# Preparing and streaming the last feed forward layer of a two layer decoder on Trainium2

## The chip, the cores and the metric

The kernel runs on one core of a Trainium2 chip. The metric is the device time of one launch in microseconds (us). The five engines with their own instruction streams are TensorE (PE in the profile, its weight loads PEld), VectorE (DVE), ScalarE (ACT), GpSimd (POOL) and SyncE (SP), which issues most transfers.

## What is computed

X holds 16 batches of 256 tokens of 128 features, 4096 tokens. Six sublayers follow each other, and each ends as x = layernorm(x + f(x)):

```
x = _layernorm(x + _L0_attn_ref(x, ...))     # self attention, 16 heads of 8
x = _layernorm(x + _L0_xattn_ref(x, ctx, ...))   # cross attention over 1601 keys of 96
x = _layernorm(x + _L0_ffn_ref(x, ...))      # experts
x = _layernorm(x + _L1_attn_ref(x, ...))     # state space
x = _layernorm(x + _L1_xattn_ref(x, ctx, ...))   # cross attention over the same keys
x = _layernorm(x + _L1_ffn_ref(x, ...))      # feed forward, below
```

The last one, which the change is mostly about, is a layer of 128 -> 512 -> 128 with quantised weights and a lora term:

```
scale = max(|W|) / 127                       # one for each of W_fc, W_proj
Wq = W + ((clip(round(W / scale), -128, 127) * scale) - W)
h = gelu(x @ Wq_fc.T + b_fc + 2 * (x @ A_fc.T) @ B_fc.T)
y = h @ Wq_proj.T + b_proj + 2 * (h @ A_proj.T) @ B_proj.T
```

## The kernel before, in words

X lies in SBUF for the whole program as 32 tiles of 128 tokens x 128 features. The program is a row of blocks, and at the end of each all engines meet. `constants` (L689) loads X in four transfers of 512 KB and makes the identities on GpSimd; its block ends when X is there. `attention` (L158) runs three times: over 256 keys of the batch itself, and twice over the 1601 keys of the context. `experts`, `state_space` and `feed_forward` (L1357) follow their attentions, and `store` (L716) writes X with one transfer.

**Attention.** A static plan (`_schedule`, L76) gives each step of a batch a slot, and every engine walks through the same plan, each picking its own steps. The batches overlap: while a batch has its scores computed (B, L493) and weighted (PV, L514), the next has its queries and keys projected (Q, K, V). Those are split into three bf16 parts (SPLIT_Q, SPLIT_K, `split`, L272; on VectorE for batch 0, on GpSimd for the others). SP writes the parts to a stacked layout by nine transfers for queries, and nine per group of keys (STACK_Q, STACK_K, L333 to L360). Row maxima come from a first set of scores (A, L461), reduced by VectorE (L649), split by GpSimd (L401 to L407), transposed (MT, L485) and inserted as rows of the queries (ROWS). BIAS (L408) adds the bias of the output projection to a batch of X on GpSimd, OX, ONT, OUT and LN end the batch. The queues of all engines are in order. SP's first steps in an attention are the weights (L318 to L324) and LOAD_X of batches 0 and 1 (L329); GpSimd's are the constants and the stacks' fill (L370 to L377).

**Feed forward.** SP loads the raw weights and small tensors by eight transfers (L1415). TensorE transposes all 32 tiles of X (L1440), and ScalarE copies them to `xT` (L1491). VectorE takes the peaks of both weights (L1518), GpSimd spreads them over the partitions (L1428), and VectorE quantises in six passes (L1522 to L1528). TensorE transposes the quantised weights by products with the identity and adds the lora products into the same bank (L1453 to L1460), and ScalarE copies the result (L1496, L1498). Then come eight blocks of 512 tokens (`block_of`, L1465): four products for the hidden features (L1469), a product of a row of ones with the bias (L1474), Gelu on ScalarE (L1503), 16 products for the output (L1479). VectorE adds X (L1533) and normalises (`layernorm`), with the root on GpSimd (L1432, L1434). The first block is written out, the others are a hardware loop:

```
pe.matmul(bank[:, m, :], w1[:, m * P:(m + 1) * P], xb, start=True, stop=True)
...
pe.wait_ge(ln_dve, (i - 1) * (1 + 3 * BT) + 1)
...
pe.matmul(bank[:, 4, t * D:(t + 1) * D], ones_row[:, :], bias2[:, :],
          start=(t == 0), stop=False, skip_group_check=True)
...
pe.wait_ge(gelus, i * FC + m + 1)
```

## Time and profile before

| | us |
|---|---|
| median of 3 runs (3863.64 to 3867.38) | 3864.87 |
| the profiled execution | 3866.06 |
| its span, first to last instruction | 3864.3 |
| self attention and what is ahead of it | 0 to 335 |
| first cross attention | to 1752 |
| experts | to 2108 |
| state space | to 2351 |
| second cross attention | to 3753.3 |
| feed forward and store | to 3864.3 |

Over the span TensorE is busy for 89%, VectorE for 74%, ScalarE for 60%, GpSimd for 28%. A stretch's row gives busy time of each engine in it and the clock that TensorE was granted, as a share of 2.4 GHz (0.50 is 1.2 GHz). A timeline's row gives the start, the duration, engine, line and operation, out<-in by the program's names, the number of instructions merged into it, and in brackets how long the engine was idle before it and for whom. Times are from the start of the span.

### The profile page before, as it was taken

The page shows a single profiled execution, that of the slowest core. Times are in us where ns is not written, and L with a number is a line of the kernel's source. Part 1 is how long each engine was busy: PE and PEld are TensorE (multiplying, and loading weights), DVE is VectorE, ACT ScalarE, POOL GpSimd, SP SyncE. Part 2 cuts the span into 40 slices and gives each one's busy share as a digit, 9 for nine tenths or more (in the row PEclk, how much of TensorE's full clock was granted, in tenths as well). Part 3 has the DMA queues.
Part 4 walks back from the last instruction along what each step waited for, and adds up shares of the span by engine and source line. Part 5 has one row for each costly group of instructions (what it writes and reads, how often), then busy time and mean ns, then how long its engine had stood idle before and what let it go on. Part 6 is the DMA issues. An engine that isn't in the chain of part 4 may idle for free. (4 is left out here: it accounts for less than half of the span.)

```text
span 3864.3 us, 97882 instructions
## 1 busy us (share of the span) xinstructions
PE 3442.3 (89%) x39003; PEld 1703.8 (44%) x39003; DVE 2871.3 (74%) x3920; ACT 2329.9 (60%) x4575; POOL 1067.8 (28%) x1874
## 2 busy tenths in 40 slices
PE   5885999999999999984999582999999999999988
PEld 3442444444444444433666581444444444444435
DVE  5776788888888888854344896888888888888852
ACT  3663677777777777771332530777777777777663
POOL 4552223222222322201665002232222223222201
PEclk9997999999999999996999795999999999999998
DMA  3332222232222223201000002222322222232200
GB/s 98 75 79 58 61 55 60 55 77 61 56 63 54 59 58 75 57 12 25 1 0 1 0 0 61 53 60 56 76 63 54 63 54 59 62 70 63 49 16 22
DMA packets 165138, 194.88 MB, mean 50 GB/s; under 512 B 32166, under 2 KB 124123, under 8 KB 164715
## 3 DMA queue, kind: packets, MB, share of 16 engines
q1 hardware_dynamic: 164714, 189.03, 20.8%
q8 instruction: 291, 4.77, 0.5%
q14 instruction: 133, 1.08, 0.1%
HBM read 27.88 MB, written 2.10 MB: 8 GB/s over the span
## 5 line engine op out<-in xcount | busy, mean ns | idle before, releaser
L586 ACT ACTIVATE cross_Pr<-cross_sT 128x512 f32<-128x512 f32 (+1 forms) x3584 | 1833.6, 563 | 768.8 <-PE cross_sT L508 767.8
L649 DVE TENSOR_REDUCE cross_nm<-cross_ring 128x2 f32<-128x802 f32 x2048 | 1975.6, 991 | 323.7 <-PE cross_ring L474 295.3
L508 PE MATMUL cross_sT<-cross_Q,cross_K 64*128 64x256 bf16 x13312 | 1044.2, 273 | 49.3 <-ACT cross_Pr L586 42.2
L527 PE MATMUL cross_oT<-cross_Pr,cross_V 128*9 128x256 f32 x13312 | 1029.8, 381 | 0.0
L508 PEld LDWEIGHTS cross_sT<-cross_Q,cross_K 64*128 64x128 bf16 x13312 | 511.1, 95 | 771.8 <-ACT cross_Pr L586 637.1
L474 PE MATMUL cross_ring<-cross_K,cross_Q 64*128 64x401 bf16 x4096 | 662.3, 337 | 62.2 <-DMA cross_K<-cross_kparts 33.5
L401 POOL TENSOR_TENSOR cross_mp<-cross_nm,cross_one 128x8 bf16<-128x8 f32 x128 | 25.9, 202 | 1373.6 <-DVE cross_nm L654 1373.6
L527 PEld LDWEIGHTS cross_oT<-cross_Pr,cross_V 128*9 128x9 f32 x13312 | 197.6, 88 | 412.6 <-issue 245.1
L474 PEld LDWEIGHTS cross_ring<-cross_K,cross_Q 64*128 64x128 bf16 x4096 | 199.0, 94 | 202.7 <-DVE cross_nm L649 106.9
L1104 DVE TENSOR_TENSOR moe_rc<-moe_r,moe_bank 128x512 f32<-128x512 f32 x128 | 87.9, 687 | 170.8 <-ACT moe_r L995 170.8
L876 POOL TENSOR_TENSOR moe_hh<-moe_r,moe_rc 128x512 f32<-128x512 f32 x128 | 162.5, 1270 | 160.0 <-DVE moe_rc L1104 159.3
L995 ACT ACTIVATE moe_r<-moe_bank 128x512 f32<-128x512 f32 x144 | 86.1, 598 | 196.1 <-PE moe_bank L934 193.8
L586 ACT ACTIVATE self_Pr<-self_sT 128x512 f32<-128x512 f32 x256 | 138.8, 594 | 84.6 <-PE self_sT L508 84.4
L658 DVE TENSOR_REDUCE self_nm<-self_ring 128x4 f32<-128x1024 f32 x128 | 155.3, 1224 | 46.0 <-PE self_ring L481 41.8
L946 PEld LDWEIGHTS moe_bank<-moe_down,moe_hh 128*128 128x128 f32 x1152 | 150.7, 191 | 55.0 <-issue 47.1
L1245 PE MATMUL ssm_bank<-ssm_diag,ssm_state 128*128 x1024 | 124.0, 281 | 56.8 <-DVE ssm_state L1343 56.8
L276 POOL TENSOR_TENSOR cross_qparts<-cross_qf,cross_one 128x256 bf16<-128x256 f32 x30 | 18.4, 612 | 514.3 <-DVE cross_qf L626 514.3
L946 PE MATMUL moe_bank<-moe_down,moe_hh 128*128 128x128 f32 x1152 | 152.4, 275 | 0.0
L934 PE MATMUL moe_bank<-moe_xT,moe_up 128*128 (+1 forms) x288 | 149.4, 601 | 1.3 <-ACT moe_cT L988 1.3
L1245 PEld LDWEIGHTS ssm_bank<-ssm_diag,ssm_state 128*128 128x128 f32 x1024 | 120.2, 196 | 60.6 <-issue 52.4
L458 PE MATMUL cross_ring<-cross_wv,cross_in 97*128 97x128 f32 (+1 forms) x832 | 124.1, 296 | 21.0 <-DVE cross_nm L649 21.0
L1343 DVE TENSOR_TENSOR_SCAN ssm_state<-ssm_decay,ssm_dtu 128x2048 f32<-128x2048 f32 x32 | 139.2, 4411 | 4.7 <-PE ssm_bank L1245 2.7
(296 smaller groups left out, 3035.7 us busy)
## 6 DMA issues: line engine op xcount, KB each, us to landing
cross_K<-cross_kparts SPq DMA_DIRECT2D x1152, 100.1 KB, 2.3
cross_in<-in_ctx_T_dram SPq DMA_DIRECT2D x32, 600.4 KB, 5.5
self_QK<-self_parts SPq DMA_DIRECT2D x144, 128.0 KB, 2.7
cross_Q<-cross_qparts SPq DMA_DIRECT2D x288, 64.0 KB, 2.1
X<-in_x_dram SPq DMA_DIRECT2D x4, 512.0 KB, 6.1
self_in<-in_x_T_dram SPq DMA_DIRECT2D x16, 128.0 KB, 2.3
cross_Q<-cross_mst SPq DMA_DIRECT2D x128, 16.0 KB, 1.8
out_dram<-X SPq DMA_DIRECT2D x1, 2048.0 KB, 8.7
```

The lines of the kernel that those rows point to most:

```text
L458: mm = pe.matmul(R[0:r, (c - lo) * D:(c - lo + 1) * D], sT_in[b % 2][:, s:s + r], wv[:, :], start=True, stop=True)
L474: mm = pe.matmul(R[:, 512 * j:512 * j + cfg.block], Q[ROWS * j:ROWS * (j + 1), pair, 0, t * P:(t + 1) * P], K[ROWS * j:ROWS * (j + 1), pai ...
L508: mm = pe.matmul(sT[0:r, cfg.sT_bank(b, u + j), (c % 2) * S:(c % 2 + 1) * S], K[ROWS * j:ROWS * (j + 1), pair, t, s:s + r], Q[ROWS * j:ROW ...
L527: mm = pe.matmul(oT[32 * j:32 * j + VR, 0:S], V[0:r, b % VB, c, 4 * g + j, :], Pr[0:r, slot, (c % 2) * S:(c % 2 + 1) * S], start=(c == 0), ...
L586: act.activation(Pr[0:r, u % NPR, 0:nc_ * S], sT[0:r, cfg.sT_bank(b, u), 0:nc_ * S], ACT.Exp).then_inc(exped, 1)
L649: dve.tensor_reduce(nm4[:, g % 2, t, :, pk, blk], R.rearrange("p (j n) -> p j n", j=2)[:, :, 0:cfg.block], AX.X, ALU.max, negate=True).the ...
L658: dve.tensor_reduce(nm[:, g % 2, :, :, a].rearrange("p t j -> p j t"), R.rearrange("p (j t n) -> p j t n", j=2, t=QT), AX.X, ALU.max, nega ...
L876: pool.tensor_tensor(hh[:, q, :], r[:, q, :], rc[:, q, :], ALU.mult).then_inc(hidden, 1)
L934: pe.matmul(bank[:, m % 2, :], up[:, m, :], xb, start=True, stop=True).then_inc(up_done, 1)
L946: mm = pe.matmul(bank[:, 4, t * D:(t + 1) * D], hh[:, m % 3, t * P:(t + 1) * P], down[:, m, :], start=(m == 0 and t == 0), stop=(m == NCH ...
L1245: return pe.matmul(bank[:, tile // BT, (tile % BT) * D:(tile % BT + 1) * D], lhs, rhs, start=first and tile % BT == 0, stop=True, skip_gro ...
L1343: dve.tensor_tensor_scan(state[:, h, :], decay[:, h, :], dtu[:, h * HALF:(h + 1) * HALF], 0.0, ALU.mult, ALU.add).then_inc(scanned, 1)
```

## The change

There are five parts; the 16 output products of a block stay as they are. The line numbers of the changed kernel differ by those added.

1. X is loaded in the self attention: two transfers of 1024 KB on SP's queue, one behind each of LOAD_X of batch 0 and 1. The first BIAS on GpSimd waits for both. `constants` loads nothing.
2. The host lays out the last layer's weights: both transposed in one tensor, the four lora matrices in another, the bias by partition. ScalarE issues the loads of both tensors in the second cross attention, behind the XT of batch 0.
3. The quantisation moves into the second cross attention: peaks on VectorE (OX of batch 4), their spreading and scaling on GpSimd (BIAS of batch 6), the reciprocal on VectorE (OX of batch 8), and the six passes over each of the two weights on GpSimd, two per BIAS of batches 9 to 14.
4. The last layer transposes a block of X one block ahead, adds the bias on GpSimd to X, copies transposed X by VectorE, adds the lora product to the weights on VectorE, has two banks for its output, and is written out without loops. A Gelu of one column comes first on ScalarE.
5. Each block of 512 tokens is stored as soon as it is normalised, and there is no block for the store.

```
@@ attention, sync @@
                         sp.dma_start(sT_in[b % 2][0:KIN, :], src_T[b]).then_inc(in_ready[b % 2], 16)
+                        if x_dram is not None and b < 2:
+                            n = NT // 2
+                            sp.dma_start(X[:, b * n:(b + 1) * n, :],
+                                         x_dram.rearrange("b (t p) f -> p (b t) f", p=P)[:, b * n:(b + 1) * n, :])\
+                              .then_inc(x_in, 16)
@@ attention, gpsimd, BIAS @@
+                        else:
+                            pool.wait_ge(x_in, 16 * 2)
...
+                        if ffn_weights is not None and b == 6:
+                            ffn_spread(ffn_weights, pool)
+                        if ffn_weights is not None and 9 <= b < 15:
+                            ffn_quantise(ffn_weights, pool, (b - 9) // 3, (b - 9) % 3)
@@ attention, scalar, XT @@
+                        if ffn_weights is not None and b == 0:
+                            ffn_load(ffn_weights, act)
@@ attention, vector, OX @@
+                        if ffn_weights is not None and b == 4 and half == 0:
+                            ffn_measure(ffn_weights, dve)
+                        if ffn_weights is not None and b == 8 and half == 0:
+                            ffn_invert(ffn_weights, dve)
@@ constants @@
-            for q in range(4):
-                n = NT // 4
-                sp.dma_start(X[:, q * n:(q + 1) * n, :],
...
-            sp.wait_ge(x_in, 16 * 4)
@@ new functions @@
+def ffn_load(fw, act):
+    weights, lora = fw.dram
+    act.dma_start(fw.raw[:, :, :], weights).then_inc(fw.loaded, 16)
+    act.dma_start(fw.lora[:, :], lora).then_inc(fw.lora_loaded, 16)
+def ffn_measure(fw, dve):
+    dve.wait_ge(fw.loaded, 16)
+    dve.tensor_reduce(fw.peak[:, :], fw.raw[:, :, :], AX.X, ALU.max, apply_absolute_value=True)\
+       .then_inc(fw.measured, 1)
+def ffn_spread(fw, pool):
+    pool.wait_ge(fw.measured, 1)
+    pool.partition_all_reduce(fw.peaks[:, :], fw.peak[:, :], P, bass.bass_isa.ReduceOp.max)\
+        .then_inc(fw.peaked, 1)
...
+def ffn_quantise(fw, pool, w, part):
...
+    if part == 0:
+        pool.wait_ge(fw.measured, 2)
+        pool.tensor_tensor(quant, raw, inverse, ALU.mult).then_inc(done, 1)
+        pool.wait_ge(done, n + 1)
+        pool.tensor_scalar(quant, quant, ROUND, -ROUND, ALU.add, ALU.add).then_inc(done, 1)
...
@@ feed_forward, sync @@
+            for i in range(NBLK):
+                sp.wait_ge(ln_dve, (i + 1) * PER)
+                sp.dma_start(out.rearrange("b (t p) f -> p (b t) f", p=P)[:, i * BT:(i + 1) * BT, :],
+                             X[:, i * BT:(i + 1) * BT, :]).then_inc(stored, 16)
+            sp.wait_ge(stored, 16 * NBLK)
@@ feed_forward, gpsimd, per block @@
+                pool.wait_ge(turned, i + 1)
+                pool.tensor_tensor(xb, xb, bias2[:, :].unsqueeze(1).broadcast_to([P, BT, D]), ALU.add)\
+                    .then_inc(biased, 1)
+                pool.wait_ge(ln_dve, i * PER + 1 + 2 * BT)
@@ feed_forward, tensor @@
+            pe.wait_ge(fw.lora_loaded, 16)
+            pe.matmul(bank[:, 5, :], lora[:, 0:D], lora[:, D:D + F], start=True, stop=True).then_inc(lora_done, 1)
+            turn(0)
+            for c in range(FC):
+                mm = pe.matmul(bank[:, 4, c * D:(c + 1) * D], lora[:, D + F + c * P:D + F + (c + 1) * P],
+                               lora[:, D + 2 * F:2 * D + 2 * F], start=True, stop=True)
...
+            for i in range(NBLK):
+                pe.wait_ge(took, i + 1)
+                for m in range(FC):
+                    pe.matmul(bank[:, m, :], w[:, 0, m * P:(m + 1) * P], xT[:, i % 2, :], start=True, stop=True)\
+                      .then_inc(hidden, 1)
+                if i + 1 < NBLK:
+                    turn(i + 1)
...
+                if i >= 2:
+                    pe.wait_ge(ln_dve, (i - 2) * PER + 1)
...
@@ feed_forward, vector @@
+            dve.wait_ge(fw.quantised, 12)
+            dve.wait_ge(lora_done, 1)
+            dve.scalar_tensor_tensor(w[:, 0, :], bank[:, 5, :], SCALING, fw.quant[:, 0, :], ALU.mult, ALU.add)\
+               .then_inc(w_ready, 1)
+            take(0)
...
+            for i in range(NBLK):
+                if i + 1 < NBLK:
+                    take(i + 1)
+                dve.wait_ge(summed, i + 1)
+                dve.wait_ge(biased, i + 1)
...
```

What moves stands in the instruction orders. SP at the start of the program, before (`x_T` is X transposed for the projections):

```order
L699 DMA X<-in_x_dram 128x8x128 x4
L694 UNCONDITIONAL_BRANCH [waits x_in]
L315 UNCONDITIONAL_BRANCH [waits barrier_Pool_Activation_PE_DVE_SP_release]
L320 DMA self_wq<-in_self_wq_dram 128x128
L320 DMA self_wk<-in_self_wk_dram 128x128
L320 DMA self_wv<-in_self_wv_dram 128x128
L320 DMA self_wo<-in_self_wo_dram 128x128
L323 DMA self_bq<-in_self_bq_dram 128x1
L324 DMA self_bo<-in_self_bo_dram 128x128
L332 DMA self_in<-in_x_T_dram 128x256 x2
L358 DMA self_QK<-self_parts 16x16x256 [waits self_split_k,self_rows_set]
```

The same place in the change:

```order
L321 DMA self_wq<-in_self_wq_dram 128x128
L321 DMA self_wk<-in_self_wk_dram 128x128
L321 DMA self_wv<-in_self_wv_dram 128x128
L321 DMA self_wo<-in_self_wo_dram 128x128
L324 DMA self_bq<-in_self_bq_dram 128x1
L325 DMA self_bo<-in_self_bo_dram 128x128
L333 DMA self_in<-in_x_T_dram 128x256
L336 DMA X<-in_x_dram 128x16x128
L333 DMA self_in<-in_x_T_dram 128x256
L336 DMA X<-in_x_dram 128x16x128
L364 DMA self_QK<-self_parts 16x16x256 [waits self_split_k,self_rows_set]
```

The four loads of X and the wait for them are gone from the front, and two loads stand between and behind the inputs of batch 0 and 1, ahead of the first stacking.

GpSimd in the second cross attention around the BIAS of batch 9, before:

```order
L405 TENSOR_TENSOR cross_mp<-cross_mres,cross_one 128x4x2
L407 TENSOR_TENSOR cross_mp<-cross_mres,cross_mp 128x4x2
L412 TENSOR_TENSOR X<-X,cross_bo 128x256
L276 TENSOR_TENSOR cross_qparts<-cross_qf,cross_one 128x256
L278 TENSOR_TENSOR cross_res<-cross_qf,cross_qparts 128x256
```

And in the change:

```order
L411 TENSOR_TENSOR cross_mp<-cross_mres,cross_one 128x4x2
L413 TENSOR_TENSOR cross_mp<-cross_mres,cross_mp 128x4x2
L420 TENSOR_TENSOR X<-X,cross_bo 128x256
L1413 TENSOR_TENSOR ffn_quant<-ffn_raw,ffn_inverse 128x512
L1415 TENSOR_SCALAR ffn_quant<-ffn_quant 128x512
L277 TENSOR_TENSOR cross_qparts<-cross_qf,cross_one 128x256
L279 TENSOR_TENSOR cross_res<-cross_qf,cross_qparts 128x256
```

Two passes of the quantiser stand between the bias and the split of the next queries; five more batches have two each at the same place.

TensorE in the last layer of the change, from its first instruction into the second block (`ident_f` as input: the transposes; before, all 32 of them stood first):

```order
L1507 MATMUL ffn_bank<-ffn_lora 128x512
L1502 MATMUL ffn_bank<-ident_f,X 128x128 x4
L1510 MATMUL ffn_bank<-ffn_lora 128x128 x4
L1517 MATMUL ffn_bank<-ffn_xT,ffn_w 128x512 x4
L1502 MATMUL ffn_bank<-ident_f,X 128x128 x4
L1528 MATMUL ffn_bank<-ffn_w,ffn_g 128x128 x16
L1517 MATMUL ffn_bank<-ffn_xT,ffn_w 128x512 x4
L1502 MATMUL ffn_bank<-ident_f,X 128x128 x4
L1528 MATMUL ffn_bank<-ffn_w,ffn_g 128x128 x16
```

The products with the bias are gone, and the transposes of the next block stand between the two sets of products.

## Rows read from the trace of the kernel before

**Rows 1.** Table of stretches: TensorE, weight loads, VectorE, ScalarE, GpSimd busy, clock, DMA.
```profile
30.00:342.00 312.00, 245.27 (x3028) 139.36 (x3028) 217.39 (x366) 180.99 (x401) 158.37 (x432) 0.98 0.28 70
...
2351.00:3753.00 1402.00, 1322.16 (x16320) 568.40 (x16320) 1128.17 (x1431) 960.38 (x1952) 343.36 (x612) 0.98 0.25 59
3753.00:3864.00 111.00, 87.88 (x453) 63.43 (x453) 33.10 (x123) 38.67 (x52) 10.24 (x19) 0.84 0.09 25
```

**Rows 2.** Timeline of the start: start, duration, engine, line, operation, [idle before].
```profile
0.72 4.04 SPq L699 DMA_DIRECT2D X<-in_x_dram  x4
...
1.70 0.29 POOL L712 TENSOR_SCALAR_AFFINE_SELECT ident_b<-ident_b 128x128 bf16<-128x128 bf16 x1
10.57 0.35 SPq L320 DMA_DIRECT2D self_wq<-in_self_wq_dram  x1
...
16.55 1.19 PE L443 MATMUL self_ring<-self_in,self_wq 128*128 128x256 f32 x2 [16.55 <-DMA self_in<-in_x_T_dram]
...
22.44 5.94 SPq L358 DMA_DIRECT2D self_QK<-self_parts  x9
...
30.43 1.03 PE L481 MATMUL self_ring<-self_QK 64*128 64x256 bf16 x8 [6.46 <-DMA self_QK<-self_parts]
```

**Rows 3.** Timeline of the last layer before its blocks, columns as in rows 2.
```profile
3753.62 6.31 PE L1440 MATMUL ffn_bank<-ident_f,X 128*128 128x128 f32 x32 [3.33 <-PEq L161]
...
3755.60 0.60 ACT L1491 ACTIVATE ffn_xT<-ffn_bank 128x512 f32<-128x512 f32 x1 [0.26 <-PE ffn_bank L1440]
...
3758.78 1.22 DVE L1518 TENSOR_REDUCE ffn_peak<-ffn_raw 128x2 f32<-128x1024 f32 x1 [5.47 <-DMA ffn_bias<-in_L_ffn_b_proj_dram]
...
3768.25 0.77 PE L1453 MATMUL ffn_bank<-ident_f,ffn_quant 128*128 128x128 f32 x2 [7.77 <-DVE ffn_quant L1528]
...
3780.55 6.55 PE L1469 MATMUL ffn_bank<-ffn_xT,ffn_w 128*128 128x512 f32 x8 [0.69 <-ACT ffn_w L1498]
...
3788.11 3.84 PE L1479 MATMUL ffn_bank<-ffn_w,ffn_g 128*128 128x128 f32 x32
```

**Rows 4.** Timeline of a block, of the last sum and of the store.
```profile
3791.79 3.60 PE L1469 MATMUL ffn_bank<-ffn_xT,ffn_w 128*128 x8
3792.12 0.69 DVE L1533 TENSOR_TENSOR ffn_y<-ffn_bank,X 128x512 f32<-128x512 f32 x1 [24.01 <-PE ffn_bank L1479]
...
3795.32 1.15 PE L1474 MATMUL ffn_bank<-ffn_bias,ones_row 1*128 1x128 f32 x8
...
3796.40 3.84 PE L1479 MATMUL ffn_bank<-ffn_w,ffn_g 128*128 128x128 f32 x32
...
3850.12 0.69 DVE L1533 TENSOR_TENSOR ffn_y<-ffn_bank,X 128x512 f32<-128x512 f32 x1 [3.69 <-PE ffn_bank L1479]
...
3853.60 1.12 DVE L1143 TENSOR_SCALAR X<-ffn_y,ffn_mv,ffn_rstd 128x128 f32 x4 [1.40 <-POOL ffn_rstd L1434]
3855.17 0.41 SPq L721 DMA_DIRECT2D out_dram<-X  x1
```

**Rows 5.** Table of stretches, columns as in rows 1: the two rises of the clock.
```profile
3758.00:3759.00 1.00, 1.00 (x7) 1.00 (x6) 0.22 (x1) 0.60 (x1) 0.00 (x0) 0.50 0.15 2
...
3786.00:3787.00 1.00, 1.00 (x3) 0.17 (x1) 0.00 (x0) 0.69 (x1) 0.00 (x0) 0.84 0.00 0
```

**Rows 6.** DMA issues by size: count, KB each, us to landing.
```profile
X<-in_x_dram SPq DMA_DIRECT2D x4, 512.0 KB, 6.1
self_in<-in_x_T_dram SPq DMA_DIRECT2D x16, 128.0 KB, 2.3
...
out_dram<-X SPq DMA_DIRECT2D x1, 2048.0 KB, 8.7
```

**Rows 7.** Costliest groups: count, busy us, mean ns, idle before.
```profile
L876 POOL TENSOR_TENSOR moe_hh<-moe_r,moe_rc 128x512 f32<-128x512 f32 x128 | 162.5, 1270 | 160.0 <-DVE moe_rc L1104 159.3
```

**Rows 8.** Waits in the second cross attention: us in total, times, longest.
```profile
POOL cross_qparts L276 <- DVE cross_qf L626: 256.9, 15, 17.9
...
ACT cross_mst L572 <- PE cross_ring L490: 43.4, 1, 43.4
```

More of the change, by code:

```diff
@@ L713, in _ @@
                                    pattern=[[-1, P]], channel_multiplier=1).then_inc(set_, 1)
-def store(nc, ctx, X, out):
-    stored = ctx.enter_context(nc.semaphore("stored"))
-    with nc.Block() as block:
-        @block.sync
-        def _(sp):
-            sp.dma_start(out.rearrange("b (t p) f -> p (b t) f", p=P), X[:, :, :]).then_inc(stored, 16)
-            sp.wait_ge(stored, 16)
 T = B * S
@@ L1359, in feed_forward @@
+def feed_forward(nc, top, X, ident_f, fw, b_fc, b_proj, out):
     with ExitStack() as ctx:
@@ L1473, in block_of @@
-                for t in range(BT):
-                    pe.matmul(bank[:, 4, t * D:(t + 1) * D], ones_row[:, :], bias2[:, :],
-                              start=(t == 0), stop=False, skip_group_check=True)
+                if i + 1 < NBLK:
+                    turn(i + 1)
+                if i == 0:
+                    pe.wait_ge(w_ready, 2)
+                if i >= 2:
+                    pe.wait_ge(ln_dve, (i - 2) * PER + 1)
                 for m in range(FC):
@@ L1527, in _, with take @@
-            link(dve.tensor_tensor(flat(tmp), flat(quant), flat(raw), ALU.subtract))
-            link(dve.tensor_tensor(flat(quant), flat(tmp), flat(raw), ALU.add))
-            assert steps[0] == QSTEPS
-            per = 1 + 3 * BT
-            with dve.Fori(0, NBLK) as i:
+            def take(i):
+                dve.wait_ge(turned, i + 1)
+                dve.tensor_copy(xT[:, i % 2, :], bank[:, 6 + i % 2, :]).then_inc(took, 1)
+            dve.wait_ge(fw.quantised, 12)
+            dve.wait_ge(lora_done, 1)
```

208 lines of the change are left out of this document (91 added, 117 removed).

## The prediction

> **What bounds the kernel now.** The table of stretches is read first [rows 1]. The 111 us of the last layer hold 88 us of TensorE work at a mean granted clock of 0.84, while the second cross attention before it has TensorE busy for 94% (1322.16 of 1402 us). So TensorE sets the pace in both. The timeline of the start comes next [rows 2]: nothing computes until the loads of X have landed, the second stage's first load is issued at 10.57 us, and TensorE begins 5.98 us later. The timeline of the last layer [rows 3] shows three parts: 38.5 us from its first transpose (3753.62) to the first sum on VectorE (3792.12); seven blocks of (3850.12 - 3792.12)/7 = 8.29 us [rows 4]; a tail of 14.2 us to the end of the span (3864.3). In a block [rows 4] TensorE has no gap: 3.53 us of up-projection (3791.79 to 3795.32), 1.08 of bias (to 3796.40) and the remaining 3.68 of down-projection. The clock rows [rows 5] say why the first part is dear: TensorE is at 0.50 (1.2 GHz) until 3759, and again from its idle wait for the quantiser until about 3786.5.
>
> The sum is made against the profiled execution, 3866.06 us outside and 3864.3 us of span. That is 1.19 us over the median of the three runs, 3864.87.
>
> **The start.** X no longer holds back the first block. GpSimd's last constant starts at 1.70 us and takes 0.29 [rows 2], so the next stage can begin near 2.4 instead of 10.57 us: 8.2 us. Its chain is unchanged in length: weights, projection, splits, stack. In SP's queue the two halves of X now lie between the loads of batch 0 and 1, and ahead of the first stacking transfers (22.44 us before, 14.3 now). The whole output, 2048 KB, lands in 8.7 us, and a quarter of X in a median of 6.1 with three more in the queue [rows 6]. An issue takes 0.35 to 0.41 us [rows 2, 4], so behind six loads of weights and one of input X is issued from about 5.5 us on, and its 2 MB are through by about 5.5 + 8.7 = 14.2, when the stacking data would only begin to move. I take **8.0** us. The ends are 8.2, and 8.2 less the half of X that might still be in the way, 4.3 us, so 3.9.
>
> **GpSimd inside the second cross attention.** Six times it gets two passes over 128x512 elements right behind the bias of a batch. A pass is nowhere in the trace in this form; the nearest row, a two-input float product of the same shape, takes 1.27 us [rows 7], so 2.5 us a step. The next thing in GpSimd's order is the split of the next queries, and for that it waited 256.9 us in 15 batches, 17.1 us each [rows 8]. The steps end over 14 us before that. The reduction over partitions and its scaling, once, lie in the same gap. I cost all at **0**. The Trainium skill (GPSIMD Engine Reference, Engine selection) says to keep elementwise work on VectorE, GpSimd being about twice as slow on two inputs. By that the move should lose: were its twelve passes on the path, 12 x 1.27 = 15 us would come back onto the sum. The trace has a wait in their place, so they are not.
>
> **VectorE and ScalarE inside it.** VectorE gets one reduction of 128x1024, 1.22 us in the stage now [rows 3], and one tiny reciprocal. TensorE may stand still behind them or have other work. Between 0 and 1.4 us; I take **0.5** lost. ScalarE issues two transfers just after it has emptied the first transposed queries, and its next instruction waited 43.4 us and more [rows 8]. Their 592 KB need under 3 us at the rate of the output's store, and lie between the context's load and the stacks. I cost that at nothing; were the stacks hit, it would be those 3 us at most.
>
> **The preparation of the last layer.** Gone are 28 of the 32 transposes ahead of it, the wait for eight loads, the quantiser's chain and 16 small products at 1.2 GHz. What is left in front of the first up-projection is one lora product of 512 columns, four transposes and four lora products of 128. A product of 512 columns has two passes: 6.55 us for eight passes at 1.2 GHz with their end, near 0.85 a pass [rows 3], so 1.7. Four transposes: the copies behind them come every 0.60 + 0.26 = 0.86 us [rows 3], so 0.85. The four small products have no row in this order. The sixteen products of the stage now take (3780.55 - 3768.25)/16 = 0.77 each with their last copy [rows 3], so 3.0 at most; if their weight loads overlap, as they do in the block, two passes of 0.21 are 1.7. I take 2.7, nearer to the row. Together 5.3 us, from 3753.6 to 3758.9. VectorE meanwhile adds the first weights (0.69) and copies the first block (0.69), which end near 3757.1, so TensorE is the later one. The first up-projection depends on the clock. In this stage it rose at 3759 after 5.4 us of unbroken work from 3753.62, and near 3786.5 after 6 us of it from 3780.55 [rows 3, 5]. If the new work from 3753.6 counts as unbroken, all eight passes run at 2.4 GHz and end at 3762.4. If only the projection does, six and a half run at 1.2 and it ends at 3765.1. Then four transposes at 0.43 and the down-projection with its latency, 4.01 (3788.11 to 3792.12): the first sum starts at 3766.8 or 3769.5. I take the middle, 3768.2, which is **23.9** earlier; the ends are 22.6 and 25.3. ScalarE loads its table for Gelu while that goes on.
>
> The Trainium skill (TensorE: Matmul & The Clock Gate, What's actually happening) says that the monitor's window runs free of the kernel, so the point of the rise varies from run to run. The two rises above, 5.4 and 6 us after the start of work, do not contradict it. Both ends stay in by the rows alone.
>
> **Seven blocks.** The bias products go (1.08) and four transposes of the next block come (0.43, not in the last block). From first to last sum: 7 x (3.53 + 3.68) + 6 x 0.43 = 53.05 instead of 58.00, so **4.95** less. The cover: VectorE needs 4.60 us from sum to written X (3850.12 to 3853.60 + 1.12) [rows 4], a copy of 0.69 and the waits, about 5.4 of the 7.64 us. GpSimd needs 1.4 for the root and 1.3 for the bias addition, which comes after the root and ends some 3 us before it is wanted. If that cover went, VectorE would have 2.2 us to lose first.
>
> **The end.** Now the store is issued 0.45 us after the last X and lands 8.7 us later. In the change seven of eight parts are stored under the blocks, and the last, 256 KB, follows the wait after some 0.15 us. Its landing is bounded by 2.3 (128 KB of input) and 6.1 (512 KB in a queue) [rows 6]. Scaling the store's 7 us of data to an eighth and keeping its other 1.7 to 2 us gives 2.8. Saved: 9.15 - 2.95 = **6.2**; with the ends 6.7 and 2.9.
> The Trainium skill (DMA: Bandwidth & Descriptors, Measured) wants transfers of 1 MiB or more. By that eight small stores would be a loss; in line, seven more fixed parts of 1.7 us would be 12 us. But each has 7.64 us before the next.
>
> **The sum.** 8.0 + 23.9 + 4.95 + 6.2 - 0.5 = 42.6 us. 3866.06 - 42.6 = 3823.5 for the profiled run, 3822.3 against the median.
>
> **The rivals.**
> 1. *The start gives its gain back.* The halves of X sit in front of batch 1 and the stacks, and the self attention waits for them, or the stage turns out to be paced by later transfers. For it: all go through one queue. Against: SP's next issue after its first loads is only at 22.44 us now, so the 2 MB have the time to pass. It costs 4 to 8 us: 3826 to 3830.
> 2. *The inserted steps disturb the cross attention.* GpSimd's order is fixed, so a slow step delays the split of queries and of maxima, and TensorE stops at the transposed maxima. With 17.1 us of cover that takes passes of over 8 us; short of that a VectorE instruction that is slowed beside GpSimd could cost 1 us or so in each of six batches. Total 3824 to 3840.
> 3. *Slower.* The clock is lost in the self attention. There TensorE had 245 of 312 us of work at a clock of 0.98 [rows 1], though it once waited 6.46 us for the stacks [rows 2]. In the last layer a wait of 7.77 us was followed by 1.2 GHz [rows 3]. If with work beginning 8 us sooner the clock falls at the first gap and does not come back, the 245 us become about 490 in a stage of 312, that is 0.57 us lost per us of stage. From 75 us at 1.2 GHz on, the whole 42.6 is gone; with the whole stage it is about 4000. Against it: the last layer, once dense, regained 2.4 GHz twice within about 6 us [rows 5].
> 4. *The change doesn't do what it says:* the last layer stays as long per block, because VectorE, with a copy more, or the GpSimd bias becomes the bound. Then the 4.95 go and perhaps 5 more: 3827 to 3832.
>
> **How the numbers follow.** The forecast has 0.76, rival 1 0.08, rival 2 0.08, rival 3 0.03, rival 4 0.05. The number is the forecast's, 3822.3. All good ends together give 3819.7 (0.2 + 1.4 + 0.5 + 0.5 less), all bad ends 3831.9 (4.1 + 1.3 + 3.3 + 0.9 more). Shifts of phase in two stages of 1400 us, which I can't cost, could be 2 us either way. So the range is 3817 to 3831, which takes in the forecast, most of rival 1 and parts of rivals 2 and 4. A measurement can tell 0.2%, about 7.7 us, from no change. Faster by more than that: 0.95. Within: 0.02, a bad rival 2 or a small rival 3. Slower: 0.03.
>
> **What would show it.** Right: a first instruction of TensorE near 8.4 us; a first VectorE sum in the last layer 14 to 16 us after its first matmul; blocks of 7.64 us; a last store landing in under 3.5 us; second cross attention within 2 us of 1402. Wrong: waits of TensorE or ScalarE for self attention's stacks longer than now; GpSimd's quantising steps ending less than 5 us ahead of the split of queries; a block over 8 us; a granted clock at 0.50 inside the self attention.

## The result, and the profile after

The changed kernel took 3814.25 us (median, 3813.41 to 3819.08), the kernel before, run beside it, 3864.26 (3857.27 to 3867.38). The ratio is 0.9876, 95% interval 0.9859 to 0.9893: faster by 1.2%, some 50 us where 42.6 were predicted. The profiled execution took 3814.54 us with a span of 3812.7, against 3866.06 and 3864.3: 51.5 us.

Both spans can be cut at the same instructions. Stage by stage, from the start times in the two timelines (us; a last X is the row of the last tiles of X that VectorE writes in a stage):

| stage, by its first and last instruction | before | after | less |
|---|---|---|---|
| to TensorE's first projection | 16.55 | 8.45 | 8.1 |
| to the first scores of self attention | 13.88 | 15.05 | -1.2 |
| rest of self attention | 311.93 | 312.85 | -0.9 |
| first cross attention, to its last X | 1396.16 | 1394.63 | 1.5 |
| to the experts' first transpose of X | 14.35 | 12.02 | 2.3 |
| experts | 355.7 | 351.5 | 4.2 |
| state space, to its last sum | 237.4 | 237.1 | 0.3 |
| second cross attention, to its last X | 1407.0 | 1406.8 | 0.2 |
| preparation, to the last layer's first sum | 39.1 | 15.3 | 23.8 |
| to its eighth sum | 58.0 | 51.7 | 6.3 |
| to the end of the span | 14.2 | 7.3 | 6.9 |

The stretches of the changed kernel that answer to [rows 1]; columns: TensorE, its weight loads, VectorE, ScalarE, GpSimd busy, clock, DMA share, GB/s.

```profile
23.00:336.00 313.00, 245.18 (x3028) 139.05 (x3028) 217.24 (x366) 181.04 (x401) 158.50 (x432) 0.99 0.27 69
2337.00:3738.00 1401.00, 1321.91 (x16320) 567.96 (x16320) 1128.16 (x1431) 960.82 (x1952) 358.21 (x622) 0.98 0.26 59
3738.00:3813.00 75.00, 66.32 (x362) 47.33 (x362) 39.07 (x124) 23.48 (x34) 19.93 (x27) 0.91 0.11 30
```

The attentions have the same work at the same clock, with 15 us more of GpSimd in the second cross attention; the last layer has shrunk from 111 to 75 us. The start (against [rows 2]):

```profile
2.57 0.40 SPq L321 DMA_DIRECT2D self_wq<-in_self_wq_dram  x1
...
6.03 0.85 SPq L336 DMA_DIRECT2D X<-in_x_dram  x1
6.93 1.98 SPq L333 DMA_DIRECT2D self_in<-in_x_T_dram  x1
8.45 1.19 PE L455 MATMUL self_ring<-self_in,self_wq 128*128 128x256 f32 x2 [8.45 <-DMA self_in<-in_x_T_dram]
9.12 0.71 SPq L336 DMA_DIRECT2D X<-in_x_dram  x1
...
14.32 5.97 SPq L364 DMA_DIRECT2D self_QK<-self_parts  x9
...
23.50 1.04 PE L493 MATMUL self_ring<-self_QK 64*128 64x256 bf16 x8 [7.65 <-DMA self_QK<-self_parts]
```

The last layer, whose row of TensorE answers to [rows 3] and [rows 4]:

```profile
3739.03 2.04 PE L1507 MATMUL ffn_bank<-ffn_lora 16*128 16x512 f32 x2 [3.32 <-PEq L161]
...
3741.00 1.11 PE L1502 MATMUL ffn_bank<-ident_f,X 128*128 128x128 f32 x4
...
3742.04 2.07 PE L1510 MATMUL ffn_bank<-ffn_lora 16*128 16x128 f32 x8
...
3744.04 5.62 PE L1517 MATMUL ffn_bank<-ffn_xT,ffn_w 128*128 128x512 f32 x8
...
3749.93 3.74 PE L1528 MATMUL ffn_bank<-ffn_w,ffn_g 128*128 128x128 f32 x32
...
3753.50 3.60 PE L1517 MATMUL ffn_bank<-ffn_xT,ffn_w 128*128 128x512 f32 x8
3753.70 0.69 DVE L1562 TENSOR_TENSOR ffn_y<-ffn_bank,X 128x512 f32<-128x512 f32 x1 [2.88 <-PE ffn_bank L1528]
...
3756.94 0.60 PE L1502 MATMUL ffn_bank<-ident_f,X 128*128 128x128 f32 x4
3757.13 1.27 POOL L1491 TENSOR_TENSOR X<-X,ffn_bias 128x512 f32<-128x512 f32 x1
...
3810.06 0.37 SPq L1478 DMA_DIRECT2D out_dram<-X  x1
```

TensorE works without a gap from 3739.03. In the stretch that answers to [rows 5] its clock rises at about 3747.9, 8.9 us later:

```profile
3747.00:3748.00 1.00, 1.00 (x2) 0.44 (x2) 0.00 (x0) 0.14 (x1) 0.00 (x0) 0.54 0.03 8
3748.00:3749.00 1.00, 1.00 (x3) 0.38 (x2) 0.00 (x0) 0.71 (x2) 0.00 (x0) 1.00 0.00 0
```

### The profile page after: what moved, and what is told of

Same layout as the page of the kernel before. It is cut to its first block and busy times, and to the rows that moved or that the text cites. A ratio compares the mean times of both kernels' runs of the same rounds, so it can differ in the third digit from the quotient of the medians.

```text
span 3812.7 us, 97480 instructions
## 1 busy us (share of the span) xinstructions
PE 3414.2 (90%) x38912; PEld 1681.8 (44%) x38912; DVE 2877.0 (75%) x3923; ACT 2315.7 (61%) x4557; POOL 1093.5 (29%) x1895
## 5 line engine op out<-in xcount | busy, mean ns | idle before, releaser
L520 PE MATMUL cross_sT<-cross_Q,cross_K 64*128 64x256 bf16 x13312 | 1043.8, 273 | 48.6 <-ACT cross_Pr L600 42.6
L277 POOL TENSOR_TENSOR cross_qparts<-cross_qf,cross_one 128x256 bf16<-128x256 f32 x30 | 18.4, 613 | 486.0 <-DVE cross_qf L640 486.0
```

The lines of the kernel that those rows point to most:

```text
L520: mm = pe.matmul(sT[0:r, cfg.sT_bank(b, u + j), (c % 2) * S:(c % 2 + 1) * S], K[ROWS * j:ROWS * (j + 1), pair, t, s:s + r], Q[ROWS * j:ROW ...
```

## The experiments

"Beside" names the kernel before, run on the same chip.

**How much is noise.** The kernel before, unchanged.

> The kernel before, unchanged, to see what one more profiled execution of the same instructions shows. From the first transpose of the first cross attention to the last X of the second one, the trace of before has 3410.6 us and that of the change 3402.0. Own theory: that stretch varies from execution to execution (where the clock rises, how long the experts' weights take to land), and here it is between 3400 and 3412, not equal to 3410.6. Rival: it is fixed by the kernel, so 3410.6 within 1 us, and the 8 us belong to the change.

3860.66 us; 18 executions of the kernel before there have a median of 3860.73 (3858.35 to 3867.61). In its profile the start, the preparation, the blocks and the tail agree with the table above within 0.2 us. Self attention took 2.9 us more, the first cross attention 2.4 less, and the experts 351.5 and not 355.7. The stretch that I had asked about took 3402.4 us, against 3410.6 in the trace of before and 3402.0 in the change's, so the rival (3410.6 within 1) fell: those stages vary by themselves. The changed kernel, once more:

> The change once more, for the comparison on the same chip. Own theory: 46 to 48 us less than before as timed beside it, 50 being what the first reference runs showed by their place in their spread; from its own stages, start 8.1, experts' weights 2.4, preparation 23.7, blocks 6.3, tail 6.9, together 47.4. Rival: the whole 50 is the change's.

3819.10 us median (3814.54 to 3825.59), ratio 0.9892 (0.9875 to 0.9908), beside 3861.34: 42.2 us less, where I had expected 46 to 48. Preparation 15.3, blocks 51.7, tail 7.3 are again the same. Over both measurements the change is worth 42 to 50 us.

**The start.** Two kernels take this part alone: before with X loaded in self attention, and the change with X loaded at the front.

```
x_only:   +  sp.dma_start(X[:, b * n:(b + 1) * n, :], ...).then_inc(x_in, 16)     # behind LOAD_X, b < 2
          -  sp.wait_ge(x_in, 16 * 4)                                           # in constants
x_front:  the same two edits backwards, on the changed kernel
```

> The kernel before with only the load of X moved behind the first weights. Own theory: the first scores come 6.9 us earlier, the self attention ends 6 us earlier, and the time is 6 us less than before, 3858. Rival: an earlier start also makes the later stages shorter; then 14 us less, 3850. The prediction had 8.0 less, 3856.

> The change with the load of X put back ahead of everything, the rest as in the change. Own theory: 6 us more than the change, 3820. Rival (an earlier start shortens the later stages too): 14 more, 3828.

x_only 3853.01 us, ratio 0.9978 (0.9968 to 0.9988), 7.7 us under the 3860.73 beside it. x_front 3822.55, 8.3 over the change's 3814.25, where I had expected 6 in both; its first projection starts at 16.51 and its last layer is the change's (15.3, 51.7, 7.3). The start is worth 8 us both ways. Of what the first projection gains, 1 us is given back at the stacks. x_front:

```profile
30.68 1.04 PE L486 MATMUL self_ring<-self_QK 64*128 64x256 bf16 x8 [6.75 <-DMA self_QK<-self_parts]
```

From the first projection to this row x_front takes 14.17 us; the change takes 15.05 and x_only 15.09. The second half of X is issued only at 9.12, since the second input's issue, behind the first half, takes 1.98 us in place of about 0.45. It is still under way when the stacking begins. How long the second half of X and the first stacking transfer take to land in the change:

```profile
DMA to landing us min/median/max: 8.7/8.7/8.7
DMA to landing us min/median/max: 3.5/3.5/3.5
```

So X lands at 17.8 us, 3.5 behind the first issue for the stacks. In `better` (below), where X comes behind the stacks, they are issued as early and land sooner, and the scores start 0.9 us earlier:

```profile
DMA to landing us min/median/max: 2.5/2.5/2.5
14.35 5.98 SPq L360 DMA_DIRECT2D self_QK<-self_parts  x9
22.59 1.04 PE L494 MATMUL self_ring<-self_QK 64*128 64x256 bf16 x8 [6.72 <-DMA self_QK<-self_parts]
```

**The second cross attention.** Is GpSimd's wait really a cover? `dose` adds passes behind each quantising step, on scratch data that nothing reads: with the step's own two there are 12 in each of batches 9 to 11 and 24 in each of 12 to 14. `quant_dve` moves the quantiser to VectorE.

```
dose:       +  for k in range(22 if w else 10):
            +      pool.tensor_tensor(tmp, raw, inverse, ALU.mult).then_inc(fw.extra, 1)
quant_dve:  -  ffn_quantise(ffn_weights, pool, (b - 9) // 3, (b - 9) % 3)     # BIAS
            +  ffn_quantise(ffn_weights, dve, (b - 9) // 3, (b - 9) % 3)      # OX
```

> The change with more GpSimd work behind the bias of a batch in the second cross attention: 10 further passes of 1.27 us in batches 9 to 11 (12 in all, 15 us) and 22 further in batches 12 to 14 (24 in all, 30 us); the further passes write a scratch tensor. Own theory: up to about 17 us the work lies in GpSimd's wait for the next queries, so batches 9 to 11 keep their 84.03 us, and each of the last three gets longer by 30.5 - 17.1 less some slack, about 12 us. Rival: any GpSimd work there slows its neighbours; then batches 9 to 11 are longer by 1 us or more as well, and the two passes of the change cost a part of that.

> The change with the six passes over each weight on VectorE, at the first OX of batches 9 to 14, not on GpSimd. A pass over half the columns takes 0.69 us there with two inputs and about 0.4 with one, 7 us in all. Own theory: VectorE has some slack against TensorE, but the ring of two buffers passes on part of it: second cross attention 2 to 5 us longer than the 1406.8 of the change. Rival (from a page's rule that VectorE is the place for elementwise work): as short or shorter than with GpSimd.

dose: 3839.4 us. With 12 passes the batches follow each other at 84.03 us as without any; with 24 the stage is 1431.3 us instead of 1406.8, 8.2 for each of the three batches, where I had expected about 12. GpSimd's rows, first the change, then dose, at the next split of the queries:

```profile
3245.47 0.61 POOL L277 TENSOR_TENSOR cross_qparts<-cross_qf,cross_one 128x256 bf16<-128x256 f32 x1 [15.26 <-DVE cross_qf L640]
```

```profile
3230.70 11.12 POOL L1432 TENSOR_TENSOR ffn_tmp<-ffn_raw,ffn_inverse 128x512 f32<-128x512 f32 x10
3245.88 0.62 POOL L277 TENSOR_TENSOR cross_qparts<-cross_qf,cross_one 128x256 bf16<-128x256 f32 x1 [4.05 <-DVE cross_qf L640]
```

The wait shrinks by what is put in (15.26 to 4.05 us for ten passes of 1.11), and the path feels the passes only when it is used up. quant_dve: 3815.03 us, stage 1406.7 us. I had expected 2 to 5 us more, and that fell: VectorE is busy for 80% of the stage, but the twelve passes, 0.43 or 0.69 us each there, cost the stage nothing. So in this kernel the choice of the engine costs nothing either way.

**The blocks.** `bias_pe` puts the bias products back on TensorE and takes the addition on GpSimd out; `unroll` is the kernel before with the hardware loop written out.

```
bias_pe:  +  for t in range(BT):
          +      pe.matmul(bank[:, 4 + i % 2, t * D:(t + 1) * D], ones_row[:, :], bias2[0:1, :], ...)
          -  pool.tensor_tensor(xb, xb, bias2[:, :].unsqueeze(1).broadcast_to([P, BT, D]), ALU.add)
unroll:   -  with pe.Fori(1, NBLK) as i:
          +  for i in range(NBLK):
```

> The change with the bias of the second product by TensorE again (four products of a row of ones with it per block), none on GpSimd. Own theory: TensorE sets the pace, a block takes 7.45 + 1.08 = 8.5 us, first to last sum 51.7 + 7.5 = 59.2, and VectorE's first write of X falls from 1.3 to 0.34 us, since GpSimd's bias pass that ran beside it is gone. Rival: the block is bound by VectorE and GpSimd already; then under 3 us more.

> The kernel before with the eight blocks of the last layer written out on all engines, nothing else. Own theory: the hardware loop and its waits against a register cost TensorE 0.2 us a block (3.44 + 3.57 in the change against 3.53 + 3.68), so first to last sum is 58.0 - 1.4 = 56.6. Rival: the missing bias products free the two other pieces; then 58.0 as before.

bias_pe: 3827.86 us, 13.3 over the change's profiled execution: 4.7 before the first sum (20.0 for 15.3; TensorE also waits for the bias to land, and starts 4.1 us after the last X and not 0.7) and 9.0 over the blocks, 60.7 against 51.7. A block in it:

```profile
3766.58 3.60 PE L1513 MATMUL ffn_bank<-ffn_xT,ffn_w 128*128 128x512 f32 x8
...
3770.02 0.60 PE L1497 MATMUL ffn_bank<-ident_f,X 128*128 128x128 f32 x4
...
3770.55 1.15 PE L1522 MATMUL ffn_bank<-ffn_bias,ones_row 1*128 1x128 f32 x8
...
3771.63 3.84 PE L1527 MATMUL ffn_bank<-ffn_w,ffn_g 128*128 128x128 f32 x32
...
3775.30 3.60 PE L1513 MATMUL ffn_bank<-ffn_xT,ffn_w 128*128 128x512 f32 x8
```

From start to start: 3.44, 0.53, 1.08 and 3.67, together 8.72 us. The change's block is 3.44, 0.44 and 3.57 (3753.50, 3756.94, 3757.38 and on), 7.45. The bias products cost 1.08 themselves and 0.1 on either side, 1.27 in all. unroll: 3860.07 us, blocks 58.0 as with the loop, where I had expected 56.6. The loop costs nothing; that theory fell, and the borders of the bias products are what is left.

**The tail.** One store of everything behind the last block:

```
one_store:  -  sp.wait_ge(ln_dve, (i + 1) * PER)          # per block
            +  sp.wait_ge(ln_dve, NBLK * PER)             # once, then one dma_start of X
```

> The change with X stored by one transfer at the end. Own theory: only the tail changes, from last sum to the end 7.3 us becomes 4.60 + 0.15 + 8.7 + 0.4 = 13.9, 6.6 us more than the change. Rival: the seven stores under the blocks cost something there; then the blocks get shorter than 51.7 us by a microsecond or more and part of the 6.6 comes back.

3819.87 us, tail 13.7 us against 7.3, blocks 51.7. The blockwise stores take nothing from the blocks and are worth 6.4 us; the block boundary that also went is the other 0.4. The landings, change and one_store:

```profile
out_dram<-X SPq DMA_DIRECT2D x8, 256.0 KB, 2.3
```

```profile
out_dram<-X SPq DMA_DIRECT2D x1, 2048.0 KB, 8.7
```

**The 2.3 us that no part of the prediction has.** Between the first cross attention and the experts TensorE waits for the experts' weights, and the first transpose of X comes 14.4 us after the last X before and 12.0 after, with the same instructions. What differs is where the buffers lie: the change allocates 17440 B of each partition ahead of them. Six kernels are the one before with so much reserved: `pad` 17440 B, in eight buffers as in the change, then one buffer of 32, 1024, 8192 or 16384 B, and `pad128` with the four smallest of the eight, 8 B each.

```
pad:     +  for k, n in enumerate((1024, 1024, 1024, 1280, 2, 2, 2, 2)):
         +      sb(f"reserved{k}", [P, n], F32)
pad32:   +  sb("reserved", [P, 8], F32)             # the other sizes likewise
pad128:  +  for k in range(4):
         +      sb(f"reserved{k}", [P, 2], F32)
```

> The kernel before with 17 KB per partition reserved in SBUF where the change holds the last layer's weights; no instruction is added. Own theory: addresses cost nothing, so 3864 us within 4. Rival: the other addresses speed up stages that the change does not touch; then about 8 us less, 3856.

> The kernel before with 32 bytes per partition reserved ahead of all stages' tensors, where the change has 17440 bytes, which is 34 x 512 + 32. From the last X of the first cross attention to the first transpose of the experts, three kernels without the reserve show 14.26 to 14.38 us and three with it 11.83 to 12.02. Own theory: what counts is where the weights' rows start relative to some larger block, so 32 bytes do it: 11.9. Rival: the place in SBUF as such, 17 KB further, does it: 14.3.

> The kernel before with 1024 B of each partition reserved ahead of the working buffers, so that every buffer lies 1024 B further. Asked: what part of the shift by 17440 B makes the experts' first transposes come 11.8 to 12.4 us after the first cross attention's last X, and not 14.3 us. 32 B did nothing. Theory A, it is the place in the large (a boundary that the weights' buffers cross, at a distance of many KB): 14.3 here. Theory B, a low-order alignment between 32 B and 1 KB: 12 here.

> The same with 8192 B reserved. Theory A with a boundary less than 8 KB off: 11.9 us; with one further off: 14.3. Theory B (low-order alignment): as with 1024 B.

> The same with 16384 B reserved, 1056 B short of what the change reserves. Theory A (a boundary within 16 KB): 11.9 us from the last X to the experts' first transpose. Theory B (the 1056 B left over matter): 14.3 us, and 12 with 1024 B.

> The kernel before with four buffers of 8 B a partition reserved, which is the part of the 17440 B that is left without its four large buffers. 1024, 8192 and 16384 B left the wait for the experts' weights at 14.2 to 14.5 us (11.8 with all 17440 B). Theory A, the small buffers shift the weights' low-order address: 12 us here, and the transfer of the last part of the weights runs at about 340 GB/s and not at 217. Theory B, it takes the large part (over 16 KB): 14.3 us.

| | pad | pad32 | pad1024 | pad8192 | pad16384 | pad128 |
|---|---|---|---|---|---|---|
| last X to the experts' first transpose, us | 11.8 | 14.3 | 14.5 | 14.4 | 14.2 | 11.7 |
| time, us | 3860.18 | 3861.83 | 3858.53 | 3864.21 | 3860.25 | 3860.44 |

The four small buffers do it, the large ones don't, and 32 B, of which I had expected it, don't either. pad32 to pad128 are one execution each, but all traces of this case divide the same way: eight kernels without the small buffers have 14.2 to 14.6 us, twelve with them 11.7 to 12.4. One us in which the last part of the weights moves, pad32 and then pad128 (last column GB/s):

```profile
1748.00:1749.00 1.00, 0.00 (x0) 0.00 (x0) 0.00 (x0) 0.00 (x0) 0.86 (x2) 0.50 1.15 220
```

```profile
1748.00:1749.00 1.00, 0.00 (x0) 0.00 (x0) 0.00 (x0) 0.00 (x0) 0.82 (x1) 0.50 1.12 340
```

The queue is as full in both and moves half as much again. The totals don't show 2.3 us (pad's ratio is 0.9995, 0.9986 to 1.0005), since other stages vary by as much. That points to a low-order address of the destination: shifts by multiples of 1024 B and one by 32 B leave the long wait, four buffers of 8 B end it. The Trainium skill (DMA: Bandwidth & Descriptors, How a descriptor splits into AXI transactions) says that a transaction has to start at a multiple of 256 B, and that a descriptor that does not start there fetches bytes which it does not use; its example of 576 B takes one transaction more for it. It says so of reads, these are writes, and the addresses were not read out; if each small buffer takes 32 B, the buffers stood 128 B off such a multiple before and on it after, and every column of the table fits. That is argued, not shown.

**Can the clock of the last layer be held?** The preparation runs 8.9 us at 1.2 GHz. `better` moves X behind the first stacks, and adds 28 bf16 products of 64 rows behind the last output projection of the cross attention; `dense` and `dense14` leave X, and put float products of 128 rows (results unused) into all four waits at the end of the last batch.

```
better:   +  pe.matmul(sT[:, k % 3, 0:S], Ks[0][0:ROWS, 0, 0, 0:P], Qs[...][0:ROWS, 0, 0, :], ...)   # x28, behind OUT
dense:    +  pe.matmul(sT[:, j % 3, 0:P], ident_f[:, :], wo[:, :], start=True, stop=True)
             # x4 behind PV, x7 behind OX, x5 behind ONT, x28 behind OUT
dense14:     # the same, x2, x3, x2, x14
```

> The change with two more edits: the halves of X are loaded behind the stacks of batches 0 and 1 instead of between the first inputs, and TensorE gets 28 products into a free bank behind the last output product of the second cross attention, so that it does not stand idle into the last layer; their results are used nowhere. Own theory: the first scores come 0.5 to 1 us earlier; the last layer begins at 2.4 GHz and its first sum comes 10 to 11 us after the last X of the attention instead of 15.3. Together 5 us less than the change, 3809. Rival: the clock falls all the same or the filler delays the end of the attention; then no difference, 3814.

> The change with TensorE kept at work over the thin end of the second cross attention: in the last batch, 4 float products of 128 rows and 128 columns behind the last weighted values, 7 behind the transposes of the outputs, 5 behind those of the scaled outputs and 28 behind the output projection, into banks that nothing reads any more, so computation of the kernel is untouched. In the run of the better version 28 bf16 products of 64 rows came too late: the clock had gone to 0.50 at 3735, in the thin 3 us before them, they ran 6.2 us instead of 3, and the clock rose only 8.7 us after the first float product behind them, as in the change (8.9 us). Theory A: the clock falls because TensorE is thin from 3732 on, and work placed there holds it at 1.00: then the 8.9 us that the change runs at 0.50 in the last layer's preparation shrink by half, the first sum comes 10.5 to 11.5 us after the last X (15.3 in the change), and the time is 4 us under the change's, near 3810 to 3812. Theory B: the clock falls near there whatever these short products do; then the fillers run at 0.50 too, end some 3 us late as in the better version, the first sum comes 18 us behind, and the time is 3817 or more.

> As the dense version, with half the products: 2, 3, 2 and 14 in place of 4, 7, 5 and 28. There each product took 0.23 us in its two passes, the last 28 took 6.42 us where the wait they cover is 3.3, and held the last layer back by 3 us, though the clock stayed at 1.00 all through. Theory A (the clock is held by work over the thin end, and what is left is the overshoot): 14 products take 3.2 us and end with the last X; the second cross attention is 0.8 us shorter than with 28 (1406.8), the first sum of the last layer comes 11.0 to 11.5 us after it (14.3 with 28, 15.3 in the change), and the median falls to 3810 or 3811, 4 us under the change. Theory B (half the work is too thin to hold the clock): it falls near the end of the cross attention, and the first sum comes 15 us or more behind, 3814 or more.

better: 3815.62 us (3814.45 to 3818.48), ratio 0.9878 (0.9862 to 0.9895), first sum 18.4 us after the last X, 3.1 later than in the change. Its filler came too late:

```profile
3735.00:3736.00 1.00, 0.69 (x3) 0.71 (x4) 0.00 (x0) 0.17 (x1) 0.00 (x0) 0.50 0.00 0
```

```profile
3736.44 6.15 PE L567 MATMUL cross_sT<-cross_Q,cross_K 64*128 64x256 bf16 x28
3742.89 2.04 PE L1513 MATMUL ffn_bank<-ffn_lora 16*128 16x512 f32 x2 [0.30 <-PEq L162]
```

The clock was down before it began, and it ran into the last layer. Nor did it bring the clock back: that rose near 3751.9, 9.0 us after the first float product behind it, and 15.5 us after the filler's start. X behind the stacks made the first scores 0.9 us earlier (14.13 us) and is no gain over self attention. The waits in which the clock is lost begin before: in the change TensorE has 1.10 us of work from 3732 to 3735. dense: 3814.14 us (3812.35 to 3815.32), ratio 0.9881 (0.9864 to 0.9897). The clock is 1.00 all through, but each product has two passes of 0.115 us, so the last 28 took 6.42 us where 3.3 were to be covered, and the first sum is at 14.3 us, where I had expected 10.5 to 11.5. dense14:

```profile
3737.00:3744.00 7.00, 6.79 (x60) 5.99 (x52) 2.29 (x10) 0.77 (x2) 0.89 (x2) 1.00 0.00 0
3744.00:3755.00 11.00, 10.70 (x61) 7.46 (x61) 2.82 (x6) 4.24 (x6) 1.41 (x3) 1.00 0.04 9
```

The first sum comes 11.2 us after the last X, 4.1 under the change, as theory A had it. The whole time does not show it: 3814.07 us (3810.39 to 3816.27), ratio 0.9873 (0.9856 to 0.9889) beside 3861.89, where I had expected 3810 or 3811. The profiled execution has 355.2 us in the experts, 3.7 more than the change's, which takes the gain away. So dense14 beats the change in the stage it edits, and not measurably in the whole.

## Why the prediction was right, and where wrong

The direction was right, and so was the mechanism of each part but for one step at the start. The size was not: the forecast was 3822.3 with a range from 3817, and 3814.25 lies below it. The steps that failed are the terms for the blocks (4.95 us, measured 6.3) and for the end (6.2, measured 6.9), the 0.5 us of disturbance that did not come, the experts' weights, which had no term (2.3), and the time before that the sum is subtracted from, which was 3.9 us above what most executions take.

- **Start**, forecast 8.0, ends 3.9 and 8.2. Measured 8.1 to the first projection, 7.7 and 8.3 for the whole time in the two kernels that isolate it. The step "its 2 MB are through by about 5.5 + 8.7 = 14.2" failed: they landed at 17.8, after the first issue for the stacks at 14.32, and the scores came 1 us later for it. That is the part of rival 1 that came true.
- **GpSimd in the cross attention**, 0. Right, and for the passes shown by the dose: the twelve take 14.3 us (0.61 to 1.95 each). The split of the queries waits 228.9 us in 15 batches where it waited 256.9 [rows 8]. The other half of these 28 us is not the passes but the reduction over partitions, of which the prediction says no more than that it lies in the same gap. It did, with 3.9 us to spare out of 17.1, once:

```profile
2897.69 0.37 POOL L1401 PARTITION_ALL_REDUCE ffn_peaks<-ffn_peak  x1 [5.45 <-issue]
2905.16 0.25 POOL L1404 TENSOR_SCALAR ffn_scale<-ffn_peaks 128x2 f32<-128x2 f32 x1 [7.11 <-issue]
2909.31 0.61 POOL L277 TENSOR_TENSOR cross_qparts<-cross_qf,cross_one 128x256 bf16<-128x256 f32 x1 [3.90 <-DVE cross_qf L640]
```

  The two instructions are busy for 0.62 us, but from the end of the bias (2892.2) to the end of the scaling 13.2 us pass. What fills them the trace does not show. By the Trainium skill (GPSIMD Engine Reference, Engine selection) VectorE should be better for the passes. Each is shorter there (0.43 or 0.69 us), and the stage was the same within 0.1 us (quant_dve).
- **VectorE and ScalarE there**, 0.5 lost. Measured 0.2 gained, within what the stage varies by, so nothing. Rival 2 did not occur.
- **Preparation**, 23.9. Measured 23.8. The lead up to the first up-projection took 5.0 us (3739.03 to 3744.04) for 5.3. The first sum came 14.67 us after the first product, for 14.6. But the clock rose neither after 5.4 to 6 us of work nor that long after the projection began; it rose after 8.9, between the two, and the middle that I took was right by luck. This was not the chance of one execution: in ten traces of kernels with the old front the clock rises 4.8 to 5.6 us after the stage's first product, in seven with the new one 8.1 to 9.0, wherever it had fallen (1.2 to 5.0 us ahead of that product in the ten, 1.3 to 8.3 in the seven). The old front is 6.3 us of transposes with 128 rows; the new one has 2 us of products with 16 rows, 1 us of such transposes and 2 us of products with 16 rows again. Whether the 16 rows delay the rise was not tried.
- **Blocks**, 4.95. Measured 6.3. The term was mis-sized in "the bias products go (1.08)": I took the start-to-start times 3.53 and 3.68 of the neighbours over unchanged, and both had 0.1 us in them that belonged to the bias products. Seven blocks are shorter by 1.27 each, and six of them longer by the new transposes (0.44).
- **End**, 6.2. Measured 6.9. The last 256 KB landed in 2.3 us, not 2.8, the time that [rows 6] show for 128 KB, so scaling from 2048 KB was too pessimistic; the store was also issued right behind the last X, without the 0.15 us that I had left.
- **What had no term.** The experts' weights landed 2.3 us sooner, which goes with where the buffers lie and could not be read from the trace of before.
- **The time before.** The forecast subtracts from a median of three executions, 3864.87; in the 40 that ran beside the later kernels the medians are 3860.7 to 3862.4. Part of the difference is seen in the profiled one, whose experts took 4.2 us longer than the change's. Its clock, back at 1.00 since 1758.8, falls again 9.3 us into the stage and stays at 0.50 for 13.7 us; in the change it falls after 11.5 us, for 6.9. The 14 us from the ninth of the stage on, before, change and dense14:

```profile
1762.00:1776.00 14.00, 14.00 (x70) 14.00 (x69) 1.38 (x2) 1.98 (x3) 0.00 (x0) 0.51 0.00 1
```

```profile
1752.00:1766.00 14.00, 12.26 (x81) 12.02 (x80) 4.54 (x7) 3.42 (x5) 0.00 (x0) 0.76 0.00 1
```

```profile
1754.00:1768.00 14.00, 14.00 (x72) 14.00 (x72) 1.66 (x3) 2.23 (x3) 0.00 (x0) 0.54 0.00 1
```

dense14 and pad8192 have this longer stage too (355.2 and 354.3 us), and the same 13.7 us at 0.50, so the change did not remove it. In the other 17 traces the stage takes 351.2 to 352.6 us and this stretch at 0.50 is 6.8 to 10.3 us long. So the longer stage goes with the clock; what sets when it falls stays open.

The parts that repeat in every run come to 8.1 - 1.0 + 2.3 + 23.8 + 6.3 + 6.9 = 46.4 us. The sum had 42.6. Of the 3.8 between them 1.35 are the borders of the bias products, 0.7 the end, 2.3 the weights and 0.5 the disturbance that did not come, less the 1 us given back at the stacks. From the 3861 that most executions of the kernel before take, 46.4 lead to 3814.6, and the forecast's 42.6 to 3818.4, within its range. So of the 8 us by which it missed, half is the time that it subtracts from and half are these terms. The agreement with 3814.25 is in part luck: the same kernel's second measurement, 3819.10 with single executions from 3814.54 to 3825.59, lies 4.5 us above this account and within the forecast's range.

Rival 3 (the clock lost in self attention) did not occur: 0.99 over the stretch. Rival 4 neither: a block has no gap on TensorE.

## What to carry to other kernels

When a short instruction is taken out of a dense stream of TensorE, price it by the period of the loop with and without it, not by its own start-to-start time, since its neighbours carry part of it. Before work is put on an engine, look for the wait of that engine behind which it would stand, and if it decides, feed it doses until the wait is gone. When a step is moved into another engine's wait, measure it from the end of what stands before it to its own end, and not by its busy time: the reduction had 0.62 us of the one and 13.2 of the other. And compare the stages that an edit doesn't touch: here they vary by 2 to 4 us between executions, so a gain of 4 us is seen in its stage and not in the total.

## What the runs showed that I had not expected

**A GpSimd pass stops a VectorE write.** Beside the bias addition of GpSimd, VectorE's four writes of X take 2.06 us instead of the 1.11 of the last block, where no such addition runs:

```profile
3801.80 1.27 POOL L1491 TENSOR_TENSOR X<-X,ffn_bias 128x512 f32<-128x512 f32 x1
3801.86 2.06 DVE L1141 TENSOR_SCALAR X<-ffn_y,ffn_mv,ffn_rstd 128x128 f32<-128x128 f32 x4 [1.41 <-POOL ffn_rstd L1496]
...
3808.93 1.11 DVE L1141 TENSOR_SCALAR X<-ffn_y,ffn_mv,ffn_rstd 128x128 f32<-128x128 f32 x4 [1.41 <-POOL ffn_rstd L1496]
```

In bias_pe, without that addition, they take 342 ns each throughout, against a mean of 544 in the change. The first write starts 0.06 us behind GpSimd's pass and takes 1.3 us, so it ends within 0.1 us of the pass; the other three take 0.33. The Trainium skill (SBUF — State Buffer, Who interferes with whom) calls the port pair of the two an exclusive lock that the loser waits out, and the rows agree. It costs nothing here, since TensorE paces the block; it is the part of rival 4 that was real.

**A filler that did not bring the clock back.** 28 bf16 products of 64 rows back to back, 6.15 us, left it at 0.50, and it rose 9.0 us after the first float product behind them, which has 16 rows, and 7.1 after the first of 128 rows, much as in the change (8.9 and 6.9). Float products of 128 rows in the earlier waits kept it at 1.00. The two fillers differ in type, rows and place, and which of these matters was not tried.

**Four small buffers ahead of it change a transfer's rate.** The last part of the experts' weights moves at 220 GB/s without them and at 340 with them. That it is the low-order address that matters is argued above and not shown.
